# Graph kernel on Trainium2: a reordered step in the relational passes, and a wait between gathers

## The reference, cut to what matters

```
h = relu(layernorm(x))
for l in range(3):                       # the relational passes
    xr  = einsum('nd,rde->rne', h, W_rel[l])      # 8 relations: 8 tables of 256
    agg = segment_sum(xr[edge_type, src], dst)
    h   = relu(agg + h @ W_root[l] + bias[l])
x = x + h
h = relu(layernorm(x)) @ Wv + bv                  # then softmax attention per
x = x + segment_sum(h[src] * attn, dst)           # destination over q[src] + k[dst]
```

## Time and profile before

| | |
|---|---|
| median of 3 runs | 5129.6 us (5125.41 to 5138.4) |
| the profiled execution: its own time | 5129.28 us |
| its span | 5127.6 us |
| busy: PE, POOL, DVE, ACT | 64%, 61%, 37%, 24% of the span |
| mean granted TensorE clock | 0.774 |

### The profile page before, as it was taken

How to read it: one execution, slowest core, us unless ns; L and a number is a source line. 1 busy time by engine, 2 the same in 40 slices (tenths; PEclk the granted TensorE clock), 3 DMA queues, 4 the chain that set the end, 5 groups by cost and what they waited for, 6 DMA issues and landing times.

```text
span 5127.6 us, 48875 instructions
## 1 busy us (share of the span) xinstructions
PE 3293.8 (64%) x14171; PEld 1990.6 (39%) x14171; DVE 1890.7 (37%) x4736; ACT 1236.4 (24%) x2949; POOL 3151.2 (61%) x3305
## 2 busy tenths in 40 slices
PE   9994777776773676777665434443344677676666
PEld 4442333333431333333332223222222555565555
DVE  4543444443542232332232122222223454544444
ACT  2220111111110111111111000000002666666665
POOL 1126666666665666666664667676764666666664
PEclk9995888878886787888787666666666878778888
DMA  6544555554653344444443333333332333333332
GB/s 210 187 183 132 190 185 191 185 186 167 204 182 129 122 144 130 141 135 139 133 142 104 99 102 106 104 103 101 106 101 77 102 103 102 101 103 102 100 100 79
DMA packets 239997, 680.99 MB, mean 133 GB/s; under 512 B 60188, under 2 KB 111988, under 8 KB 215028
## 3 DMA queue, kind: packets, MB, share of 16 engines
q0 software_dynamic: 152400, 419.03, 28.0%
q1 hardware_dynamic: 73256, 245.85, 13.0%
q10 hardware_dynamic: 14076, 12.93, 0.9%
HBM read 501.99 MB, written 175.58 MB: 132 GB/s over the span
## 4 chain that ended last, share of the span: by engine, by line
another core or an unknown queue 31%; PE 29%; issue 14%; POOL 12%; DVE 6%; DMA 6%; ACT 2%; DVEq 1%; POOLq 0%; ACTq 0%; SPq 0%
PE bank L1661 18%; POOL ring L676 12%; DMA ring<-h_table,code 5%; PE pair_ps L1755 4%; PE both_sums L1769 4%; DVE root L941 2%; PE turn_root L1646 1%; ACT stage L1509 1%; PE bank L1798 0%; ACT xT L1447 0%; PE turn_root L1661 0%; DVE z L1235 0%; DVEq L940 0%; DVE z L907 0%
## 5 line engine op out<-in xcount | busy, mean ns | idle before, releaser
L676 POOL DMA_INDIRECT ring<-table,code x2361 | 2327.0, 986 | 1225.8 <-issue 733.7
L1661 PE MATMUL bank<-wide,xT 128*128 128x512 f32 x2352 | 1181.9, 660 | 206.9 <-ACT xT L1447 145.9
L676 POOL DMA_INDIRECT ring<-h_table,code x787 | 747.9, 950 | 461.4 <-issue 249.8
L1661 PEld LDWEIGHTS bank<-wide,xT 128*128 128x128 f32 x2352 | 489.1, 215 | 850.6 <-issue 660.7
L1769 PE MATMUL both_sums<-masks 128*128 128x256 f32 x2058 | 550.4, 426 | 320.2 <-issue 174.7
L1503 ACT COPY masks<-pair_ps 128x512 f32<-128x512 f32 x297 | 173.2, 583 | 2143.0 <-remote 1480.6
L1769 PEld LDWEIGHTS both_sums<-masks 128*128 128x128 f32 x2058 | 445.6, 219 | 416.7 <-issue 341.6
L1866 PE MATMUL pair_ps<-ring,stage 128*128 x1764 | 519.6, 445 | 98.1 <-ACT stage L1583 97.2
L1755 PE MATMUL pair_ps<-ring,masks 128*32 128x256 f32 x4722 | 450.3, 478 | 127.5 <-DMA ring<-table,code 76.6
L1646 PE MATMUL turn_root<-ident,z 128*128 128x128 f32 x392 | 104.1, 356 | 564.3 <-DVE z L1235 247.9
L1866 PEld LDWEIGHTS pair_ps<-ring,stage 128*128 128x128 f32 x1764 | 380.9, 229 | 159.1 <-issue 104.7
(11 more groups left out here) (247 smaller groups left out, 2841.2 us busy)
## 6 DMA issues: line engine op xcount, KB each, us to landing
table<-stage SPq DMA_DIRECT2D x144, 1024.0 KB
back<-table SPq DMA_DIRECT2D x49, 1024.0 KB
ring<-table,code POOLq DMA_INDIRECT x2361
ring<-h_table,code POOLq DMA_INDIRECT x787
h_table<-stage SPq DMA_DIRECT2D x49, 130.0 KB
back<-h_table ACTq DMA_DIRECT2D x49, 130.0 KB
features<-xT SPq DMA_DIRECT2D x49, 128.0 KB, 4.0
first_T<-features SPq DMA_DIRECT2D x49, 128.0 KB
```

Source lines behind the costliest of these rows:

```text
L676: pool.indirect_dma_start(slot(c % RING, width), None, table, bass.IndirectOffsetOnAxis(ap=code[:, c:c + 1], axis=0)).then_inc(landed[n % ...
L1661: last = nc.tensor.matmul(bank[q][:, 0:width], xT[:, b, k, :], weights[:, k, 512 * q:512 * q + width], start=(k == 0), stop=(k == K - 1))
```

## The change

In the relational passes the list of a step becomes, on PE: turn of i - 1, sum of tile i, all new windows of tile i + 1, and the transform (or `to_h`) of i - 1 last. The windows of tile 0 go ahead of the loop. In `transform` the root bank comes first. PE waits before the turn until DVE has emptied the root bank. ACT keeps the pairs of tile i + 1 in the same place, and DVE empties the transform of i - 1 after z of i and the masks; it adds the root bank to the bias first and the self-loops onto that. On POOL, the three relational passes get the wait for the landing of the group before, ahead of each fourth group.

```
-                    if l == L and n and n % 2 == 0:
+                    if n and n % (2 if l == L else 4) == 0:
                         pool.wait_ge(landed[(n - 1) % RINGS], 16 * gathers_to(l, n - 1))
...
             def evacuate(l, i, use, b, first=False, bias_at=False):
                 if not first:
+                    dve.wait_ge(transformed[b], CREDIT + NB * use + 1)
+                    nc.vector.tensor_tensor(root[:, i, :], bank[NB - 1][:, 0:D], bias_row[:, :], ALU.add
+                                            ).then_inc(evacuated[NB - 1], 1)
                     add_loops(l, i, use, b, range(0, R - 2))
...
                 add_loops(l, i, use, b, range(R - 2, R))
-                dve.wait_ge(transformed[b], CREDIT + NB * use + NB)
-                settle(dve, loops_done((l - 1) * NT + i, R))
-                dve.wait_ge(root_step, loops_done((l - 1) * NT + i, R))
-                nc.vector.tensor_tensor(root[:, i, :], bank[NB - 1][:, 0:D], root[:, i, :], ALU.add
-                                        ).then_inc(evacuated[NB - 1], 1)
...
                     upcoming_masks(l, i + 2)
                     if l == 0 and i + 1 < NT:
                         add_first_loops(i + 1, (i + 1) // 2, 1 - b)
-                    next_table(l, i, j, b)
+                    if i:
+                        next_table(l, i - 1, (i - 1) // 2, 1 - b)
+                next_table(l, NT - 1, PAIRS, 0)
...
+                keep_pairs(l, new_pairs(0))
                 for i in range(NT + 1):
-                    early, late = new_pairs(i) if i < NT else ((), ())
-                    keep_pairs(l, early)
                     if i:
                         relu_turned(use, b, transformed[b], NB * use)
-                    keep_pairs(l, late)
+                    if i + 1 < NT:
+                        keep_pairs(l, new_pairs(i + 1))
...
+                sum_windows(l, new_pairs(0))
                 for i in range(NT + 1):
-                    early, late = new_pairs(i) if i < NT else ((), ())
-                    sum_windows(l, early)
                     if i:
                         j, b = divmod(i - 1, 2)
+                        pe.wait_ge(evacuated[NB - 1], CREDIT + (l + 1) * NT + i - 1)
                         turn_sum(l, j, b)
-                    sum_windows(l, late)
-                    if i:
-                        transform((l + 1) * NT + i - 1, (l + 1) * USES[b] + j, b, AHEAD + REST)
                     if i < NT:
                         sum_tile(l, i, i // 2, i % 2)
+                    if i + 1 < NT:
+                        sum_windows(l, new_pairs(i + 1))
+                    if i:
+                        transform((l + 1) * NT + i - 1, (l + 1) * USES[b] + j, b, ROOT_FIRST)
...
             for i in range(NT + 1):
-                early, late = new_pairs(i) if i < NT else ((), ())
-                sum_windows(L - 1, early)
                 if i:
                     turn(L * USES[b] + j, b)
-                sum_windows(L - 1, late)
+                if i < NT:
+                    sum_tile(L - 1, i, i // 2, i % 2)
+                if i + 1 < NT:
+                    sum_windows(L - 1, new_pairs(i + 1))
                 if i:
                     to_h(j, b)
-                if i < NT:
-                    sum_tile(L - 1, i, i // 2, i % 2)
```

More of the change, by code:

```diff
@@ L94, in new_pairs @@
     def new_pairs(t):
-        pairs = range(pairs_to(t - 1), pairs_to(t))
-        half = (len(pairs) + 1) // 2
-        return pairs[:half], pairs[half:]
+        return range(pairs_to(t - 1), pairs_to(t))
     assert WINDOW * GROUP == P and pairs_to(NT - 1) == NP and GROUPS >= SPAN
@@ L912, in evacuate @@
                 if not first:
+                    dve.wait_ge(transformed[b], CREDIT + NB * use + 1)
+                    nc.vector.tensor_tensor(root[:, i, :], bank[NB - 1][:, 0:D], bias_row[:, :], ALU.add
+                                            ).then_inc(evacuated[NB - 1], 1)
                     add_loops(l, i, use, b, range(0, R - 2))
-                dve.wait_ge(transformed[b], CREDIT + NB * use + q + 1)
+                dve.wait_ge(transformed[b], CREDIT + NB * use + (q + 1 if first else q + 2))
                 dve.wait_ge(stored[b], table_stored(l, b, use))
@@ L937, in add_loops @@
                         dve.wait_ge(evacuated[t // 2], CREDIT + l * NT + i + 1)
-                    if t:
+                    if t == 0:
+                        dve.wait_ge(evacuated[NB - 1], CREDIT + l * NT + i + 1)
+                    else:
                         settle(dve, loops_done((l - 1) * NT + i, t))
@@ L941, in add_loops @@
                     nc.vector.scalar_tensor_tensor(root[:, i, :], bank[t // 2][:, t % 2 * D:(t % 2 + 1) * D], loop_weight(i, t),
-                                                   root[:, i, :] if t else bias_row[:, :], ALU.mult, ALU.add
+                                                   root[:, i, :], ALU.mult, ALU.add
                                                    ).then_inc(root_step, 1)
@@ L1227, in conv_head @@
                     dve.wait_ge(evacuated[q], CREDIT + NT * (l + 1))
+                if l:
+                    dve.wait_ge(root_step, loops_done((l - 1) * NT + NT - 1, R))
                 with dve.If(nb > 0):
@@ L1531, in _ @@
             conv_head(L - 1)
+            keep_pairs(L - 1, new_pairs(0))
             for i in range(NT + 1):
-                early, late = new_pairs(i) if i < NT else ((), ())
-                if i:
-                    deviation(NT + i - 1)
-                keep_pairs(L - 1, early)
                 if i:
@@ L1539, in _ @@
                     relu_turned(L * USES[b] + j, b, h_ready[b], j)
-                keep_pairs(L - 1, late)
+                if i < NT:
+                    deviation(NT + i)
+                if i + 1 < NT:
+                    keep_pairs(L - 1, new_pairs(i + 1))
             def lower_score(c, i, b):
@@ L1650, in transform @@
                 found = None
-                if banks[0] == 0:
+                if banks[0] in (0, NB - 1):
                     pe.wait_ge(xT_ready[b], use + 1)
@@ L1669, in _ @@
             AHEAD = list(range(NB - 2))
-            REST = list(range(NB - 2, NB))
-            FIRST_REST = REST[:-1]
+            FIRST_REST = [NB - 2]
+            ROOT_FIRST = [NB - 1, *range(NB - 1)]
             def tile_before_layers(j, b):
@@ L1800, in to_h @@
                 last.then_inc(h_ready[b], 1)
+            sum_windows(L - 1, new_pairs(0))
             for i in range(NT + 1):
-                early, late = new_pairs(i) if i < NT else ((), ())
-                sum_windows(L - 1, early)
                 if i:
```

3 lines of the change are left out of this document (1 added, 2 removed).

## The result

The changed kernel takes 5162.1 us (median of 5 runs, 5157.4 to 5177.8) against 5129.6 us before (5 runs): ratio 1.0069, 95% interval 1.0052 to 1.0085. It is slower by 0.7%, where 1.4% faster was forecast. The profiled execution took 5161.7 us, its span 5159.9.

What follows compares the result with a forecast made beforehand. POOL's gathers, held up by ring waits, were taken to bound the relational passes. Ring waits -354 + 35, landing waits +273 and pass ends -23 gave -69 us: 5060 us, 1.4% faster, with an 8 in 10 range of 4990 to 5220.

Steps and rivals of the forecast that it cites:

- the first and largest term: POOL's ring waits in the relational passes: the new order on PE removes 354 us, of which 35 us may stay.
- nothing comes of it: Rival: PE's word grows later, POOL still meets the full ring, new waits lie inside old ones: 5145 us; chance 0.15.
- The landing waits: POOL's 147 new waits in the relational passes, 1.86 us each above the usual start: +273 us, bounds 0 and 403.
- that lower bound: POOL's new landing waits cost 0 where POOL would have stood still for the ring anyway.
- The two large terms: In the relational passes: ring waits, -354 us with 35 staying, and POOL's new landing waits, +273 us.
- The ends of the passes: Gaps between last and first gather, two passes: 43 us each expected, -23 us together, bounds -39 and +16.
- PE should now be close behind the landings: At a pass's end: PE no longer four tiles behind; gap of 35 us, or 43 with PE one tile behind.
- the new wait of the turn ... nothing: PE's turn waits for the root bank of i - 2 to be empty, work a step old: no cost.
- SP's store of a tile goes out a step later ... nothing, except at the end of a pass: SP's later store of a table tile runs beside gathers: no cost, except at the end of a pass.
- The third end: After the third pass, to_h and DVE's chain after the last sum stay as before: 0 us.
- slower gathers: Relational gathers take 986 ns, 92 us in all over the shortest, 947; forecast to stay, no change.
- The slower rival: POOL pays landing waits and ring waits both: 5418 us, or 5260 with half the pauses releasing; chance 0.23.

Runs made afterwards that it cites:

- e17: The changed kernel without the new landing waits of the relational passes, on a late chip: 5140.4 us against 5128.1 us for the kernel before, ratio 1.0016.
- e2: The changed kernel without the new landing waits of the relational passes, on a prompt chip: 4731.7 us against 4717.9 us for the kernel before, ratio 1.0030.
- e15: The kernel before with only the new landing waits of the relational passes added, on a late chip: 5154.8 us against 5126.4 us, ratio 1.0065.
- e8: Changed kernel without new landing waits; in the first pass SyncE's store a step later, VectorE's loops behind the evacuation; prompt chip: 4726.8 us against 4716.7 us before, 1.0021.
- e5: The changed kernel, unaltered, timed again on a late chip: 5230.3 us against 5202.8 us for the kernel before, ratio 1.0056.
- e6: Changed kernel, its new landing waits asking for the group two before instead of the last; late chip: 5226.3 us against 5202.8 us before, ratio 1.0056.
- e18: Kernel before, with PE's relational window sums multiplying a constant row instead of the gathered rows, on a late chip: 5132.7 us against 5128.1 us, ratio 1.0011.
- e16: The kernel before without the attention's 98 landing waits, on a late chip: 5194.6 us against 5126.4 us, ratio 1.0135.
- e9: The kernel before without the attention's 98 landing waits, on a prompt chip: 4539.6 us against 4716.7 us, ratio 0.9627.
- e1: The kernel before with only the new landing waits of the relational passes added, on a prompt chip: 4989.5 us against 4717.9 us, ratio 1.0574.

## Why the prediction was wrong

**The step that failed** is the first and largest term: "so the 354 us of ring waits should go almost wholly", 35 left. The new order alone (e17) leaves 398.1 us of the 395.3. I had reasoned that PE's word is late by a fixed time and that 9.5 us of transform put behind sum and windows would lie beside it. The delay is not a time that PE's later work can run beside. PE's own queue is held up as well: in the step shown above the windows crawl, and the transform starts when the word is through. The page's row of the window matmuls shows it for all passes: the kernel before and the one after, then e17 and e2, which are the same kernel on a late and on a prompt chip.

```profile
L1755 PE MATMUL pair_ps<-ring,masks 128*32 128x256 f32 x4722 | 450.3, 478 | 127.5 <-DMA ring<-table,code 76.6
```

```profile
L1757 PE MATMUL pair_ps<-ring,masks 128*32 128x256 f32 x4722 | 624.9, 434 | 609.1 <-issue 407.0
```

```profile
L1757 PE MATMUL pair_ps<-ring,masks 128*32 128x256 f32 x4722 | 576.4, 414 | 541.8 <-issue 458.1
```

```profile
L1757 PE MATMUL pair_ps<-ring,masks 128*32 128x256 f32 x4722 | 441.6, 472 | 1075.9 <-DMA ring<-table,code 1055.6
```

On late chips PE stands idle before the windows of the new order for over 400 us that the profile puts to no wait, on the prompt one for 4, and there it waits for the gathers as it should. In the old order PE stood before the turn instead, 564.3 us in all, 247.9 of them for z. What was queued behind the delay did not hide it. The third pass had nearly the same ring waits with little more than half of PE's work; that spoke for this, and I had it in the text, under the rival "nothing comes of it".

**The landing waits** were sized rightly for a kernel without ring waits: +273 forecast, +271.6, 273.3 and 268.8 measured on three prompt chips. In the profile at hand they were not to be added, since POOL would have stood still anyway: +28 us on the late chip (e15). I had named that lower bound and taken the full price, because I had already struck the ring waits out. The two large terms were both wrong, in opposite directions, so that their sum is off by less than either: -46 forecast for both, +37 in the trace after. The Trainium skill (DMA: Bandwidth & Descriptors, Rules for kernel authors) has the rule to wait on a transfer's semaphore late; prompt chips agree, with 271.6 us for 147 early waits, and the late chip only with 28.

**The ends of the passes**: -23 us forecast, +24.1 in the trace after (+20.9 and +3.2), beyond the bound of +16. Two steps of it failed. "PE should now be close behind the landings" rested on the ring waits going. And "the new wait of the turn ... nothing" and "SP's store of a tile goes out a step later ... nothing, except at the end of a pass" overlooked the chain store, load back, loops, root bank, turn, which exists in the first pass alone. On prompt chips the order costs 12.2 and 7.1 us at the two ends; 7.4 of the 12.2 hang on this chain (e8); the 7.1 are of the size of the transform, which the prediction priced at 7.83. On a late chip the chain was not tried by itself. The third end, put at 0, became 11.6 us shorter; why was not traced.

**No change** for slower gathers was off by little: 974 ns for 986, -27 us. On the late chips the waits in the old order give 977 ns (e15) and the new order without them 983 (e17), so most of it comes with the waits.

**The rivals.** "Nothing comes of it", 5145 us, came nearest: full ring in each tile, new waits for the most part inside old ones, more work at the ends. Its reason, a delay that grows, is borne out in part: the middle z is late by 4.95 us before, by 5.28 with the order alone (e17) and by 7.27 with order and waits. Its price was 17 us short. The first pass and its end hold 26 us that it did not count, the second and third pass 10, and the third end gives 12 back; how much of the 26 is the chain is open on late chips. The slower rival ("the pause is paid and the ring wait stays", 5418 or 5260) did not happen: the sum of both kinds of waits rose by 37 us, not by 273.

**How the 0.7% divides on late chips**: the order alone 1.0016 (e17, +12 us), the waits alone 1.0065 (e15, +28 us), both 1.0069 and 1.0056. On the chip of e5 and e6, where the waits cost next to nothing, the order should have most of its 27 us. So the share of each differs from one late chip to another, and the runs don't allow a finer split.

**Open.** What holds PE and its word back on some chips was not found. In the rows read it follows PE's instructions, and while POOL's gathers stream; it is not PE's reading of the ring (e18), and it is not the program alone, since the same program shows it on one chip and not on another. The mean granted clock of the kernel before was 0.797 to 0.810 on the prompt chips and 0.769 to 0.782 on the late ones of e5, e15 and e17; by itself a clock that is 3% lower does not make z start 5 us after its sum. Whether PE's signals come late or its instructions reach it late was not separated: the crawl inside a group, where no signal is waited for, speaks for the second at least in part. That more gathers in flight make it dearer, as e16 suggests, was not tested in the relational passes.

## What to carry to other kernels

Before moving work to hide a late signal, ask whether the engine whose signal is late still makes progress behind it; look in the timeline at the instructions queued next, not only at the one that waits. If they crawl too, work queued behind the delay will not hide it, and waits put elsewhere may fall into it or be paid in full.

Leaving out the attention's landing waits gained 3.7 and 3.8% on two chips and cost 1.4% on a third. Run a change of waits on several chips, with the kernel before beside it, ahead of settling on it.

Where a store is moved a step later, follow each load that stands behind it in the same queue to the engine that waits for it.

## What the runs showed of the hardware

The same program takes 4717.9, 4716.7 and 4714.7 us on three chips, and 5126.4, 5128.1, 5129.6 and 5202.8 in the other four groups of runs. The 412 us between 5129.6 and 4717.9 are for the most part the 354 us of ring waits above the usual start and the first two ends of a pass, shorter by 15.6 and 16.1 us (40.04 and 36.89 us in e9, against the earlier trace rows). The page's row of ACT's copies of the window sums tells them apart at a glance: in e1 their idle time ends with PE's instruction, on a late chip with the same kernel (e15) for the most part with "remote".

```profile
L1503 ACT COPY masks<-pair_ps 128x512 f32<-128x512 f32 x297 | 173.4, 584 | 2105.9 <-PE pair_ps L1755 2105.9
```

```profile
L1503 ACT COPY masks<-pair_ps 128x512 f32<-128x512 f32 x297 | 173.6, 585 | 2112.0 <-remote 1461.9
```

The mean gather takes 977 ns in either run: its own time doesn't tell the chips apart.

A late chip's trace also holds fewer updates of semaphores. Of the 50368 that the landings of 3148 gathers make (16 each), 13642 are in the trace of the kernel before and 50246 in that of e1. So "remote" and "issue" in a late chip's trace can also mean that a record is missing, and the split between landing and ring waits is less certain there than their sum. The starts and idle times, on which the readings above rest, come from the instructions' own records.
